# Column attention, first of four stages: symmetric scores from the diagonal on, x transposed by DMA, and the splitting of x spread over three engines

## The chip, the core and the metric

The program runs on one core of one Trainium2 chip. The metric is the device time of one execution in microseconds (us). An engine is called by the name of the profile: PE (TensorE matmul; PEld are its weight loads), DVE (VectorE), ACT (ScalarE), POOL (GpSimd), SP (SyncE, which only issues DMAs here).

## What is computed

Input x is 8 x 512 x 512 in float32. Four blocks follow, each of the form x = x + layernorm(block(layernorm(x))). The change is in the first block:

```python
scores = jnp.einsum('bci,bcj->bij', x, x)
weights = jax.nn.softmax(scores, axis=-1)
context = jnp.einsum('bij,bcj->bci', weights, x)
```

Each batch's score matrix is symmetric. The second block multiplies by the sum over eight 512 x 512 factors, and the first stage sums those factors on the side. The third block is grouped attention, the fourth a gated feed-forward layer.

## The kernel before

A batch is 4 tiles (T = 4) of 128 rows x 512 columns. Every product is made to nearly float32 accuracy by splitting each operand into a high part (fp32r, a rounded copy) and a low part (what is left), and adding three products: `products` (L57) issues 12 matmuls per output tile, three pairs for each of four blocks of the contraction.

`column_attention` is the first stage. Per batch b it makes the normalised xn (DVE, L335), its high part xh (DVE, L341) and low part xl (POOL, L231). PE makes four score tiles of 128 x 512 from them, in two PSUM banks used in turn (`score[t % 2]`). For each score tile DVE takes the row maximum, ACT the exponential, DVE the reciprocal of the row sum, POOL multiplies (prob, L236). PE transposes xn and prob in blocks of 128 x 128 into `turned` (L439), ACT takes the high part out of PSUM (xth, pth), DVE the low part (xtl, ptl, L357). From these PE makes four context tiles. For the residual, DVE takes the statistics of the context tiles (obn, omv), POOL turns them into a scale and a shift (`row_scales`, four small instructions), ACT applies them (normed, L301), POOL adds to x (L247). DVE also adds one 1 MB factor to `factor_sum` in each batch (L391).

Each engine has its own written-out order, and semaphores join them. A batch's context tiles run one batch behind its scores. Of a loop over pairs of batches (`over_batches`) PE, DVE and SP execute the body; ACT and POOL run their last steps two batches behind. DMAs are issued on SP alone. Within a batch PE's order is: score tile and transposes of xn, four times, then context tile of the batch before and transposes of prob, four times. The context buffers are four PSUM banks, so context tile t of a batch waits until ACT has read tile t of the batch before.

## Time and profile before

| | us |
|---|---|
| median of 3 runs (1651.66 to 1653.26) | 1653.04 |
| the profiled execution | 1653.88 |
| its span, first to last instruction | 1652.0 |
| PE busy / DVE busy / POOL busy in the span | 1498.8 / 1048.3 / 733.4 |

The times in the rows are counted from the first instruction of the span. Durations in a trace overlap for matmuls, since they are pipelined: what a matmul costs is read from start to start, not from its length. The first stage takes some 257 us of the span; the other three follow and are not changed.

### The profile page before, as it was taken

The page shows a single profiled execution, that of the slowest core. Times are in us where ns is not written, and L with a number is a line of the kernel's source. Part 1 is how long each engine was busy: PE and PEld are TensorE (multiplying, and loading weights), DVE is VectorE, ACT ScalarE, POOL GpSimd, SP SyncE. Part 2 cuts the span into 40 slices and gives each one's busy share as a digit, 9 for nine tenths or more (in the row PEclk, how much of TensorE's full clock was granted, in tenths as well). Part 3 has the DMA queues.
Part 4 walks back from the last instruction along what each step waited for, and adds up shares of the span by engine and source line. Part 5 has one row for each costly group of instructions (what it writes and reads, how often), then busy time and mean ns, then how long its engine had stood idle before and what let it go on. Part 6 is the DMA issues. An engine that isn't in the chain of part 4 may idle for free.

```text
span 1652.0 us, 22026 instructions
## 1 busy us (share of the span) xinstructions
PE 1498.8 (91%) x7332; PEld 1214.2 (73%) x7332; DVE 1048.3 (63%) x2091; ACT 789.7 (48%) x1506; POOL 733.4 (44%) x914
## 2 busy tenths in 40 slices
PE   4999996995899999999999998579899999999996
PEld 3777775874687877778787876467688888888885
DVE  4698846874888888888888778545424334234233
ACT  1333334644877878687878777321212222222121
POOL 3486742663444545454545445213243333333331
PEclk9999997997999999999999999889999999999998
DMA  4121102224000202020202020222110110100100
GB/s 152 52 102 51 50 1 71 76 89 141 1 1 1 77 1 77 2 77 1 77 1 77 1 96 1 83 96 90 33 51 1 51 51 0 51 32 18 51 26 26
DMA packets 41797, 80.00 MB, mean 48 GB/s; under 512 B 2416, under 2 KB 3440, under 8 KB 41712
## 3 DMA queue, kind: packets, MB, share of 16 engines
q1 hardware_dynamic: 41712, 78.93, 13.7%
q8 instruction: 46, 0.75, 0.2%
q14 instruction: 39, 0.32, 0.1%
HBM read 53.75 MB, written 25.17 MB: 48 GB/s over the span
## 4 chain that ended last, share of the span: by engine, by line
PE 57%; DVE 10%; POOL 4%; issue 3%; ACT 3%; DMA 1%; SPq 0%; POOLq 0%; DVEq 0%; ACTq 0%
PE f_inner L57 22%; PE g_side L1381 12%; PE f_down L1792 9%; PE g_score L57 5%; PE g_turned L1401 5%; DVE g_ptl L1305 2%; PE g_output L1427 2%; PE g_output L1429 2%; DVE g_neg_max L1291 2%; DVE f_wl L1716 1%; POOL g_prob L1016 1%; PE f_inner L1764 1%; POOL g_power L990 1%; DVE g_q L1220 1%; ACT g_pth L1167 1%
## 5 line engine op out<-in xcount | busy, mean ns | idle before, releaser
L1016 POOL TENSOR_SCALAR g_prob<-g_prob,g_inv_sum 128x512 f32<-128x512 f32 x256 | 178.7, 698 | 308.4 <-DVE g_inv_sum L1296 308.4
L57 PE MATMUL f_inner<-f_xth,f_wh 128*128 128x512 f32 x704 | 281.3, 400 | 15.8 <-DVE f_wl L1716 12.7
L57 PE MATMUL f_inner<-f_xtl,f_wh 128*128 128x512 f32 x704 | 279.5, 397 | 0.0
L1685 DVE SCALAR_TENSOR_TENSOR f_hidden<-f_inner,f_inner_scale,f_silu 128x512 f32<-128x512 f32 x88 | 66.0, 750 | 313.8 <-PE f_inner L57 313.8
L1574 POOL TENSOR_TENSOR f_hl<-f_hidden,f_hh 128x512 fp32r<-128x512 f32 x88 | 128.1, 1456 | 296.8 <-DVE f_hh L1691 296.8
L1626 ACT ACTIVATE f_silu<-f_inner,f_inner_scale 128x512 f32<-128x512 f32 x88 | 60.7, 690 | 413.8 <-PE f_inner L57 413.8
L1291 DVE TENSOR_REDUCE g_neg_max<-g_score 128x1 f32<-128x512 f32 x256 | 175.4, 685 | 83.9 <-PE g_score L57 82.7
L1125 ACT ACTIVATE g_prob<-g_score,g_neg_max 128x512 f32<-128x512 f32 x256 | 177.0, 691 | 96.9 <-DVE g_neg_max L1291 94.7
L1305 DVE TENSOR_TENSOR g_ptl<-g_turned,g_pth 128x512 fp32r<-128x512 f32 x256 | 173.8, 679 | 15.6 <-ACT g_pth L1167 13.6
L1401 PE MATMUL g_turned<-identity,g_prob 128*128 128x128 f32 x1024 | 155.2, 274 | 27.1 <-DVE g_ptl L1305 27.0
L57 PEld LDWEIGHTS f_inner<-f_xth,f_wh 128*128 128x128 f32 x704 | 133.1, 189 | 54.6 <-DVE f_wl L1716 17.5
L1167 ACT CAST g_pth<-g_turned 128x512 fp32r<-128x512 f32 x256 | 149.5, 584 | 46.7 <-PE g_turned L1401 44.6
L1401 PEld LDWEIGHTS g_turned<-identity,g_prob 128*128 128x128 f32 x1024 | 121.3, 140 | 64.3 <-issue 34.4
L57 PEld LDWEIGHTS f_inner<-f_xtl,f_wh 128*128 128x128 f32 x704 | 133.2, 189 | 31.7
L1792 PE MATMUL f_down<-f_wh,f_hh 128*128 128x512 f32 x352 | 140.1, 398 | 0.9 <-POOL f_hl L1574 0.9
L1792 PE MATMUL f_down<-f_wh,f_hl 128*128 128x512 f32 x352 | 139.3, 396 | 0.0
L57 PE MATMUL g_score<-g_kh,g_q 128*128 128x512 f32 x256 | 122.2, 478 | 2.7 <-DVE g_q L1220 2.7
L1427 PE MATMUL g_output<-g_pth,g_v 128*128 128x512 f32 x256 | 101.0, 395 | 1.6 <-DVE g_ptl L1305 1.6
L57 PE MATMUL g_score<-g_kl,g_q 128*128 128x512 f32 x256 | 100.9, 394 | 0.0
L1429 PE MATMUL g_output<-g_ptl,g_v 128*128 128x512 f32 x256 | 100.6, 393 | 0.0
L1792 PEld LDWEIGHTS f_down<-f_wh,f_hh 128*128 128x128 f32 x352 | 66.3, 188 | 16.9 <-POOL f_hl L1574 1.3
L1792 PEld LDWEIGHTS f_down<-f_wh,f_hl 128*128 128x128 f32 x352 | 66.4, 189 | 15.5
(200 smaller groups left out, 3460.3 us busy)
## 6 DMA issues: line engine op xcount, KB each, us to landing
x_resident<-x SPq DMA_DIRECT2D x8, 1024.0 KB, 7.0
x_mixed<-x_resident SPq DMA_DIRECT2D x8, 1024.0 KB, 4.4
x_pair<-x_mixed SPq DMA_DIRECT2D x8, 1024.0 KB, 7.8
g_res<-x_mixed SPq DMA_DIRECT2D x8, 1024.0 KB, 6.1
x_attended<-g_res SPq DMA_DIRECT2D x8, 1024.0 KB, 5.1
x_pair<-x_attended SPq DMA_DIRECT2D x8, 1024.0 KB, 5.7
factor<-factors SPq DMA_DIRECT2D x7, 1024.0 KB, 5.2
out<-x_pair SPq DMA_DIRECT2D x7, 1024.0 KB, 4.3
```

What stands on the lines that cost most here:

```text
L57: last = nc.tensor.matmul(out, lhsT, rhs, start=(n == 0), stop=(n == len(pairs) - 1))
L1016: nc.gpsimd.tensor_scalar(prob[:, at, :], prob[:, at, :], inv_sum[:, at:at + 1], 1.0, ALU.mult, ALU.mult).then_inc(prob_ready, 1)
L1125: nc.scalar.activation(prob[:, at, :], score[u % 2][:, :], ACT.Exp, bias=neg_max[:, at:at + 1], scale=1.0, accum_out=row_sum[:, at:at + 1] ...
L1167: nc.scalar.copy(pth[:, (turn_u // T) % 2, :, at * P:(at + 1) * P], blocks_of(turned[turn_u % 2][:, :])).then_inc(hi_ready, 1)
L1291: nc.vector.reduce_max(neg_max[:, at:at + 1], score[u % 2][:, :], AX, negate=True).then_inc(max_ready, 1)
L1305: nc.vector.tensor_tensor(ptl[:, at, :, cols], blocks_of(turned[turn_u % 2][:, :]), pth[:, at, :, cols].bitcast(F32), ALU.subtract).then_i ...
L1381: last = nc.tensor.matmul(out[:, bank_cols], *pairs[n], start=(k == 0 and n == 0), stop=(k == T - 1 and n == 2))
L1401: mm = nc.tensor.transpose(turned[turn_u % 2][:, cols], prob[:, turn_u % 4, cols], s.identity[:, :])
L1427: nc.tensor.matmul(output[hd % 2][:, :], lhsT, pth[:, hd % 2, t, :], start=(t == 0), stop=False)
L1429: mm = nc.tensor.matmul(output[hd % 2][:, :], lhsT, ptl[:, hd % 2, t, :], start=False, stop=(t == T - 1))
L1574: nc.gpsimd.tensor_tensor(hl[:, at, :], hidden[:, at, :], hh[:, at, :].bitcast(F32), ALU.subtract).then_inc(hl_ready, 1)
L1792: last = nc.tensor.matmul(down[t][:, :], l[:, at, cols], r[:, i, 2, :], start=(i == 0 and n == 0), stop=(i == IT - 1 and n == len(halves) ...
```

## The change

The names and lines are those of the new kernel. A DRAM input `x_t` holds each batch transposed; it is made ahead of the run.

- Scores: tile t is computed only from column 128 t on (512, 384, 256, 128 columns). ACT copies what stands right of the diagonal block into SBUF (`upper`), and PE transposes those blocks into the columns left of the diagonal of later tiles (1, 2 and 3 transposes).
- xn is not stored. ACT makes xh from x directly (scale and shift in one activation); POOL makes `scaled` = x times scale; DVE makes xl = scaled + shift - xh in one instruction with two SBUF inputs.
- The transposes of xn on PE, with their PSUM reads, go. `x_t` comes by DMA in two halves per batch into `xt`; ACT makes xth, DVE makes xtl from `xt` and xth, both in SBUF.
- A factor is loaded and added in two halves. The residual's statistics and scales go by pairs of tiles. The context of a batch is normed one batch behind instead of two. PE's order interleaves score and context tiles. The loops are written out.

The diff, cut to its core (removed bodies stand in the listing above):

```diff
-        xn = sb("xn", [P, 2, T, N])
+        scaled = sb("scaled", [P, T, N])
+        xt = sb("xt", [P, T, N])
...
         prob = sb("prob", [P, T, N])
+        upper = [sb(f"upper{t}", [P, N - (t + 1) * P]) for t in range(T - 1)]
         normed = sb("normed", [P, 2, N])
-        factor = sb("factor", [P, T, N])
...
+            load_x(0)
+            for b in range(B):
+                if b < B - 1:
+                    sp.wait_ge(x_loaded, b * 16 + 16)
+                    load_x(b + 1)
+                for h in range(2):
+                    load_half(b, h)
...
                 else:
...
-
+                    for h in range(2):
+                        if b > 1 or h > 0:
+                            sp.wait_ge(factor_used, b * 2 - 2 + h)
+                        sp.dma_start(factor[:, :, :], rows_of(factors, b)[:, 2 * h:2 * h + 2, :]).then_inc(factor_loaded, 16)
         @block.gpsimd
...
+                nc.gpsimd.tensor_scalar(raw_eps[:, b % T, :], mv[:, :, 1], EPS, EPS, ALU.add, ALU.mult)
...
+            def scaled_x(b, tiles):
+                if tiles[0] == 0:
+                    pool.wait_ge(scales, b + 1)
...
+                    nc.gpsimd.tensor_scalar(scaled[:, t, :], s.x[:, b * T + t, :], rs[:, t:t + 1], 1.0,
+                                            ALU.mult, ALU.mult).then_inc(scaled_ready, 1)
...
+            def output_scales(b, h):
+                half = slice(2 * h, 2 * h + 2)
+                pool.wait_ge(ostats, b * 2 + h + 1)
...
             scales_of(0)
...
+            scaled_x(0, range(T))
+
+            def body(b, p, first, last):
+                if b >= 2:
+                    add(b - 2, 0)
+                    output_scales(b - 2, 1)
+                    add(b - 2, 1)
+                    add(b - 2, 2)
+                probabilities(b, p, 0)
+                if last:
+                    following.row_scales(nc, s, pool)
+                else:
+                    scales_of(b + 1)
+                probabilities(b, p, 1)
                 if not last:
-                    for t in range(T):
-                        lo_of(b + 1, 1 - p, t)
-
-            over_batches_two_behind(pool, body)
-            output_scales(B - 2)
-            for t in range(T):
+                    scaled_x(b + 1, (0, 1, 2))
+                probabilities(b, p, 2)
+                if not last:
+                    scaled_x(b + 1, (3,))
+                if b >= 2:
+                    add(b - 2, 3)
+                if not first:
+                    output_scales(b - 1, 0)
+                probabilities(b, p, 3)
...
+            def hi_of_xn(b, p, t):
+                if t == 0:
+                    act.wait_ge(scales, b + 1)
+                    if b >= 2:
+                        act.wait_ge(scored, (b - 1) * T)
+                nc.scalar.activation(xh[:, p, t, :], s.x[:, b * T + t, :], ACT.Identity, bias=shift[:, t:t + 1],
+                                     scale=rs[:, t:t + 1]).then_inc(xh_ready, 1)
+
+            def copy_upper(b, t):
+                act.wait_ge(scored, b * T + t + 1)
+                nc.scalar.copy(upper[t][:, :], score[t % 2][:, (t + 1) * P:]).then_inc(copied, 1)
...
+            def hi_of_xt(b, p, t):
+                if t % 2 == 0:
+                    act.wait_ge(xt_loaded[t // 2], b * 16 + 16)
...
+                nc.scalar.copy(xth[:, p, t, :], xt[:, t, :]).then_inc(xth_ready, 1)
...
+            def body(b, p, first, last):
+                hi_of_xt(b, p, 0)
+                hi_of_xt(b, p, 1)
+                copy_upper(b, 0)
+                if not first:
+                    hi_of_prob(b - 1, 1 - p, 2)
+                    hi_of_prob(b - 1, 1 - p, 3)
+                if b >= 2:
+                    norm(b - 2, 2)
+                exp(b, p, 0)
+                copy_upper(b, 1)
+                if b >= 2:
+                    norm(b - 2, 3)
+                exp(b, p, 1)
+                copy_upper(b, 2)
+                if not last:
+                    hi_of_xn(b + 1, 1 - p, 0)
+                exp(b, p, 2)
+                if not last:
+                    hi_of_xn(b + 1, 1 - p, 1)
+                hi_of_prob(b, p, 0)
+                if not last:
+                    hi_of_xn(b + 1, 1 - p, 2)
+                hi_of_prob(b, p, 1)
+                exp(b, p, 3)
+                if not last:
+                    hi_of_xn(b + 1, 1 - p, 3)
+                if not first:
+                    norm(b - 1, 0)
+                    norm(b - 1, 1)
+                hi_of_xt(b, p, 2)
+                hi_of_xt(b, p, 3)
+                if last:
+                    hi_of_prob(b, p, 2)
+                    hi_of_prob(b, p, 3)
...
+            def lo_of_xn(b, p, t):
+                dve.wait_ge(scaled_ready, b * T + t + 1)
+                dve.wait_ge(xh_ready, b * T + t + 1)
+                nc.vector.scalar_tensor_tensor(out=xl[:, p, t, :], in0=scaled[:, t, :], scalar=shift[:, t:t + 1],
+                                               in1=xh[:, p, t, :].bitcast(F32), op0=ALU.add,
+                                               op1=ALU.subtract).then_inc(xl_ready, 1)
+
+            def lo_of_xt(b, p, t):
+                dve.wait_ge(xth_ready, b * T + t + 1)
+                nc.vector.tensor_tensor(xtl[:, p, t, :], xt[:, t, :], xth[:, p, t, :].bitcast(F32),
+                                        ALU.subtract).then_inc(xtl_ready, 1)
...
             def maximum(b, p, t):
                 dve.wait_ge(scored, b * T + t + 1)
+                if t < T - 1:
+                    dve.wait_ge(copied, b * (T - 1) + t + 1)
                 nc.vector.reduce_max(neg_max[:, p * T + t:p * T + t + 1], score[t % 2][:, :], AX,
                                      negate=True).then_inc(max_ready, 1)
...
+                if t % 2 == 1:
+                    h = t // 2
+                    tile.then_inc(own_obn, 1)
+                    dve.wait_ge(own_obn, b * 2 + h + 1)
+                    if b > 0:
+                        dve.wait_ge(oscales, b * 2 + h - 1)
+                    for t in (2 * h, 2 * h + 1):
                         last = nc.vector.bn_aggr(omv[:, t, :], obn[:, t, :])
                     last.then_inc(ostats, 1)
...
+            def add_factor(b, h):
+                dve.wait_ge(factor_loaded, 16 + ((b - 1) * 2 + h + 1) * 16)
+                half = s.factor_sum[:, 2 * h:2 * h + 2, :]
+                nc.vector.tensor_tensor(half, half, factor[:, :, :], ALU.add).then_inc(factor_used, 1)
...
             def body(b, p, first, last):
...
+                if b >= 2:
+                    output_stats(b - 2, 3)
                 if not last:
-                    hi_of_xn(b + 1, 1 - p)
-                for t in range(T):
-                    if not first:
-                        output_stats(b - 1, t)
-                    lo_of(b, p, T + t)
-
-            over_batches(dve, body)
-            dve.wait_ge(added, T + 2)
-            following.statistics(nc, dve, [s.x[:, t, :] for t in range(T)])
-            for t in range(T):
+                    tile_stats(b + 1, 0)
+                    tile_stats(b + 1, 1)
+                    tile_stats(b + 1, 2)
+                if not first:
+                    lo_of_prob(b - 1, 1 - p, 2)
+                    lo_of_prob(b - 1, 1 - p, 3)
+                maximum(b, p, 0)
+                if not last:
+                    tile_stats(b + 1, 3)
+                    stats_of(b + 1)
+                if last:
+                    dve.wait_ge(added, T)
+                    following.statistics(nc, dve, [s.x[:, t, :] for t in range(T)])
+                inverse(b, p, 0)
+                maximum(b, p, 1)
+                lo_of_xt(b, p, 0)
+                if not first:
+                    output_stats(b - 1, 0)
+                    add_factor(b, 0)
+                inverse(b, p, 1)
+                lo_of_xt(b, p, 1)
+                maximum(b, p, 2)
+                if not last:
+                    lo_of_xn(b + 1, 1 - p, 0)
+                inverse(b, p, 2)
+                if not last:
+                    lo_of_xn(b + 1, 1 - p, 1)
+                if not first:
+                    output_stats(b - 1, 1)
+                lo_of_prob(b, p, 0)
+                maximum(b, p, 3)
+                lo_of_prob(b, p, 1)
+                if not last:
+                    lo_of_xn(b + 1, 1 - p, 2)
+                inverse(b, p, 3)
+                if not last:
+                    lo_of_xn(b + 1, 1 - p, 3)
+                if not first:
+                    output_stats(b - 1, 2)
+                lo_of_xt(b, p, 2)
+                lo_of_xt(b, p, 3)
+                if not first:
+                    add_factor(b, 1)
+                if last:
+                    lo_of_prob(b, p, 2)
+                    lo_of_prob(b, p, 3)
...
+            written_out(body)
+            output_stats(B - 2, 3)
+            for t in range(T - 1):
                 output_stats(B - 1, t)
-
-            for t in range(T):
-                dve.wait_ge(ctx_normed, B * T + t + 1)
-                x = tile_of(s.x, (B - 1) * T + t)
-                nc.vector.tensor_tensor(x, x, normed[:, t % 2, :], ALU.add).then_inc(last_added, 1)
+            add_last(0)
+            add_last(1)
+            output_stats(B - 1, 3)
+            add_last(2)
+            add_last(3)
 
...
                 if not (first and t < 2):
                     pe.wait_ge(exp_ready, b * T + t - 1)
...
+                if t > 0:
+                    pe.wait_ge(copied, b * (T - 1) + t)
+                for r in range(t):
+                    nc.tensor.transpose(score[t % 2][:, block_at(r)], upper[r][:, block_at(t - r - 1)],
+                                        s.identity[:, :])
+                products(nc, score[t % 2][:, t * P:],
+                         [(l[:, p, k, block_at(t)], r[:, p, k, t * P:])
                           for k in range(T) for l, r in ((xh, xh), (xl, xh), (xh, xl))]).then_inc(scored, 1)
...
+                pe.wait_ge(prob_ready, b * T + g + 1)
...
                 if t == 0:
-                    pe.wait_ge(lo_ready, (b + 1) * 8)
-                pe.wait_ge(ctx_normed, b * T + t + 1)
-                at = slice(t * P, (t + 1) * P)
+                    pe.wait_ge(xtl_ready, (b + 1) * T)
+                    pe.wait_ge(lo_ready, (b + 1) * T)
+                if b > 0:
+                    pe.wait_ge(ctx_normed, (b - 1) * T + t + 1)
...
+                scores(b, p, 0, first)
+                if not first:
+                    turn(b - 1, 1 - p, 2, b == 1)
+                    turn(b - 1, 1 - p, 3, b == 1)
+                scores(b, p, 1, first)
+                if not first:
+                    contexts(b - 1, 1 - p, 0)
+                scores(b, p, 2, first)
+                if not first:
+                    contexts(b - 1, 1 - p, 1)
+                turn(b, p, 0, first)
+                scores(b, p, 3, first)
+                turn(b, p, 1, first)
+                if not first:
+                    contexts(b - 1, 1 - p, 2)
+                if last:
+                    turn(b, p, 2, first)
+                    turn(b, p, 3, first)
+                if not first:
+                    contexts(b - 1, 1 - p, 3)
+
+            written_out(body)
             for t in range(T):
```

In the order of instructions, DVE in the middle of a steady batch stood like this before (`xn` and `xtl` belong to the next batch and this one):

```order
L391 TENSOR_TENSOR factor_sum<-factor_sum,factor 128x2048
L350 RECIPROCAL inv_sum<-row_sum 128x1
L345 TENSOR_REDUCE neg_max<-score 128x1
L354 REGISTER_ALU
L357 TENSOR_TENSOR xtl<-turned,xth 128x4x128
L335 TENSOR_SCALAR xn<-x_resident,mv,rs 128x512 x2
L350 RECIPROCAL inv_sum<-row_sum 128x1
```

And now, from the statistics of the first context tile on:

```order
L437 BN_STATS obn<-context 128x6
L451 TENSOR_TENSOR factor_sum<-factor_sum,factor 128x1024
L427 RECIPROCAL inv_sum<-row_sum 128x1
L415 TENSOR_TENSOR xtl<-xt,xth 128x512
L422 TENSOR_REDUCE neg_max<-score 128x1
L409 SCALAR_TENSOR_TENSOR xl<-scaled,shift,xh 128x512
L427 RECIPROCAL inv_sum<-row_sum 128x1
L409 SCALAR_TENSOR_TENSOR xl<-scaled,shift,xh 128x512
L437 BN_STATS obn<-context 128x6
L445 BN_AGGR omv<-obn 128x2 x2
```

The factor's addition is halved, and instructions that read two SBUF operands (xtl, xl) stand between the maxima and the reciprocals.

POOL, from the second probability tile of a steady batch to the fourth, now stands like this (before, an addition to x followed each probability tile, and four `xl` ended the batch):

```order
L249 TENSOR_SCALAR prob<-prob,inv_sum 128x512
L244 TENSOR_SCALAR scaled<-x_resident,rs 128x512 x3
L249 TENSOR_SCALAR prob<-prob,inv_sum 128x512
L244 TENSOR_SCALAR scaled<-x_resident,rs 128x512
L265 TENSOR_TENSOR x_resident<-x_resident,normed 128x512
L255 TENSOR_TENSOR ove<-omv,raw_eps 128x2
L256 TENSOR_SCALAR oshift<-omv 128x2
L258 TENSOR_TENSOR ors<-ove,minus_half 128x2
L260 TENSOR_TENSOR oshift<-oshift,ors 128x2
L249 TENSOR_SCALAR prob<-prob,inv_sum 128x512
```

The scales of the first pair of context tiles (ove to oshift) now stand behind the scaled tiles and ahead of the last probability tile.

## Rows read from the trace of the kernel before

**Rows 1.** Busy time by window, one batch: length, engines, PE clock, DMA share, GB/s.

```profile
125.80:152.50 26.70, 26.11 (x129) 21.10 (x128) 22.93 (x42) 10.20 (x20) 19.26 (x20) 1.00 0.22 79
```

**Rows 2.** Timeline of PE in a steady batch: start, us, what.

```profile
72.07 0.60 PE L439 MATMUL turned<-identity,prob 128*128 128x128 f32 x4
72.43 0.48 PE L57 MATMUL score<-xh 128*128 128x512 f32 x1
72.74 0.39 PE L57 MATMUL score<-xh,xl 128*128 128x512 f32 x1
...
75.28 0.60 PE L439 MATMUL turned<-identity,xn 128*128 128x128 f32 x4
```

**Rows 3.** Timeline of PE in the third stage: fp32r matmuls with 128 moving columns.

```profile
398.04 0.28 PE L1381 MATMUL g_side<-g_wvl,g_hth 128*128 128x128 f32 x1
...
402.95 0.28 PE L1381 MATMUL g_side<-g_wvh,g_htl 128*128 128x128 f32 x1
```

**Rows 4.** Groups by line in 20 to 250 us: busy, mean ns, idle before.

```profile
L335 DVE TENSOR_SCALAR xn<-x_resident,mv,rs 128x512 f32 x24 | 26.1, 1126 | 1.6 <-POOL shift L108 1.6
L282 ACT ACTIVATE prob<-score,neg_max 128x512 f32<-128x512 f32 x32 | 22.1, 692 | 21.0 <-DVE neg_max L345 21.0
L345 DVE TENSOR_REDUCE neg_max<-score 128x1 f32<-128x512 f32 x32 | 21.7, 678 | 27.2 <-PE score L57 27.2
L292 ACT CAST pth<-turned 128x512 fp32r<-128x512 f32 x32 | 18.8, 587 | 60.4 <-PE turned L439 60.4
L391 DVE TENSOR_TENSOR factor_sum<-factor_sum,factor 128x2048 f32<-128x2048 f32 x7 | 16.0, 2282 | 0.0
```

**Rows 5.** Instructions of POOL's lines L236 and L247: count, ns min/median/max.

```profile
L236 POOL TENSOR_SCALAR prob<-prob,inv_sum x32: 687/702/1802, 29.9 to 220.4; 128x512 f32<-128x512 f32 x32
L247 POOL TENSOR_TENSOR x_resident<-x_resident,normed x28: 1269/1447/1468, 85.1 to 239.0; 128x512 f32 x16, 128x512 f32<-128x512 f32 x12
```

**Rows 6.** Timeline of DVE and POOL where both use SBUF.

```profile
161.52 2.28 DVE L391 TENSOR_TENSOR factor_sum<-factor_sum,factor 128x2048 f32<-128x2048 f32 x1
161.71 2.18 POOL L104 TENSOR_SCALAR shift<-mv 128x4 f32<-128x4 f32 x1
...
138.59 1.29 POOL L247 TENSOR_TENSOR x_resident<-x_resident,normed 128x512 f32 x1
138.62 2.40 DVE L335 TENSOR_SCALAR xn<-x_resident,mv,rs 128x512 f32 x2 [0.26 <-POOL shift L108]
```

**Rows 7.** Timeline of the start: DVE, and PE's first matmuls of batches 0, 1, 7.

```profile
7.43 2.47 DVE L324 BATCH_NORM_STATS2 bn<-x_resident 128x6 f32<-128x512 f32 x4 [7.43 <-DMA x_resident<-x]
...
12.38 1.91 DVE L335 TENSOR_SCALAR xn<-x_resident,mv,rs 128x512 f32<-128x512 f32 x4 [2.07 <-POOL shift L108]
...
19.28 0.76 PE L57 MATMUL score<-xh 128*128 128x512 f32 x1 [19.28 <-POOL xl L231]
24.54 1.05 PE L439 MATMUL turned<-identity,xn 128*128 128x128 f32 x4
...
44.56 0.79 PE L57 MATMUL score<-xh 128*128 128x512 f32 x1 [3.03 <-POOL xl L231]
...
205.73 0.47 PE L57 MATMUL score<-xh 128*128 128x512 f32 x1
```

**Rows 8.** Windows: the first score tile of batch 1, and the initial loads.

```profile
44.50:49.60 5.10, 5.04 (x12) 3.94 (x13) 0.00 (x0) 0.00 (x0) 0.00 (x0) 0.52 0.01 3
...
8.00:20.00 12.00, 0.72 (x2) 0.66 (x3) 6.74 (x18) 0.00 (x0) 6.19 (x6) 1.00 0.72 262
```

**Rows 9.** Timeline of the stage's end and the start of the second stage.

```profile
235.32 0.77 PE L57 MATMUL context<-pth,xth 128*128 128x512 f32 x1 [3.70 <-ACT normed L301]
...
248.50 0.39 PE L57 MATMUL context<-ptl,xth 128*128 128x512 f32 x1
...
252.09 2.99 ACT L301 ACTIVATE normed<-context,oshift,ors 128x512 f32<-128x512 f32 x4 [13.51 <-POOL oshift L108]
257.05 1.97 PE L695 MATMUL turned<-identity,xn 128*128 128x128 f32 x8 [8.16 <-ACT xn L574]
```

More of the change, by code:

```diff
@@ L166, in column_attention @@
         shift = sb("shift", [P, T])
+        raw_eps = sb("raw_eps", [P, T, T])
         obn = sb("obn", [P, T, 6])
@@ L244, in add @@
             def add(b, t):
-                pool.wait_ge(ctx_normed, b * T + t + 1 + T)
-                x = tile_of(s.x, b * T + t)
+                pool.wait_ge(ctx_normed, b * T + t + 1)
+                x = s.x[:, b * T + t, :]
                 nc.gpsimd.tensor_tensor(x, x, normed[:, t % 2, :], ALU.add).then_inc(added, 1)
             scales_of(0)
-            for t in range(T // 2):
-                lo_of(0, 0, t)
-            pool.sem_inc(xl_ready, T // 2)
-            def body(b, p, before, last):
-                if before == 2:
-                    output_scales(b - 2)
-                for t in range(T):
-                    normalise(b, p, t)
-                    if t == 0 and not last:
-                        scales_of(b + 1)
-                    if before == 2:
-                        add(b - 2, t)
-                if not last:
-                    for t in range(T):
-                        lo_of(b + 1, 1 - p, t)
@@ L318, in _, with tile_stats @@
+            written_out(body)
+            norm(B - 2, 2)
+            norm(B - 2, 3)
+            for t in range(T):
+                norm(B - 1, t)
         @block.vector
         def _(dve):
-            def stats_of(b, p):
-                dve.wait_ge(x_loaded[p], (b - p) * 8 + 16)
-                for t in range(T):
-                    last = nc.vector.bn_stats(bn[:, t, :], tile_of(s.x, b * T + t))
-                last.then_inc(own_bn, 1)
-                wait_alone(dve, s, own_bn, b + 1)
+            def tile_stats(b, t):
+                if t == 0:
+                    dve.wait_ge(x_loaded, b * 16 + 16)
+                tile = nc.vector.bn_stats(bn[:, t, :], s.x[:, b * T + t, :])
+                if t == T - 1:
+                    tile.then_inc(own_bn, 1)
@@ L360, in output_stats, with lo_of_prob @@
-            def output_stats(b, t):
-                dve.wait_ge(ctx_ready, (b + 1) * T + t + 1)
-                last = nc.vector.bn_stats(obn[:, t, :], context[t][:, :])
-                if t == T - 1:
-                    last.then_inc(own_obn, 1)
-                    wait_alone(dve, s, own_obn, b + 1)
-                    for t in range(T):
+            def lo_of_prob(b, p, g):
+                dve.wait_ge(hi_ready, b * T + g + 1)
+                nc.vector.tensor_tensor(ptl[:, p, :, block_at(g)], blocks_of(turned[g % 2][:, :]),
+                                        pth[:, p, :, block_at(g)].bitcast(F32), ALU.subtract).then_inc(lo_ready, 1)
```

202 lines of the change are left out of this document (75 added, 127 removed).

## The prediction

> **What bounds the kernel now.** I cut the first stage into batches by busy time per window, then read PE's timeline, the groups by line and the timelines of the other engines around them. In a steady batch PE is busy 26.1 of 26.7 us, DVE 22.9, POOL 19.3, ACT 10.2 [rows 1]. So PE ends the batch, with DVE close behind: only what shortens PE counts, and only until DVE or POOL ends last. Between the first score tiles of batches 1 and 7 lie 161.2 us for six batches, 26.9 each [rows 7].
>
> PE's costs are read from start to start. A 128 x 512 fp32r matmul takes 0.231 us (11 from 72.74 to 75.28), 0.31 as the first of a tile behind transposes; four transposes take 0.36 us [rows 2]. A tile is 12 matmuls, 2.85 us, and 3.2 with its transposes; eight make 25.7 us. With 128 moving columns a matmul takes (402.95 - 398.04)/44 = 0.112 us [rows 3].
>
> **PE in the new kernel.** The widths 384 and 256 do not occur in this trace. They lie between 0.112 and 0.231 us; the straight line between these gives 0.191 and 0.151, which I take since both ends are measured and the cost cannot grow with fewer columns. A batch is then:
> - scores: 12 x (0.231 + 0.191 + 0.151 + 0.112) = 8.2 us, where 11.1 were;
> - six transposes out of `upper`: 6 x 0.09 = 0.5;
> - context tiles: 48 x 0.231 = 11.1; first matmuls behind a switch, 8 x 0.08 = 0.6;
> - four transposed prob tiles 4 x 0.36 = 1.4; the four of xn are gone.
>
> Sum 21.8 us, with 20.4 to 24.7 as ends (all three narrow widths at 0.112, or at 0.231).
>
> The Trainium skill ("TensorE: Matmul & The Clock Gate", back-to-back issue gap) gives N/2.4 + 2.5 ns for an isolated matmul, 56 ns at 128 columns, and 81 ns in a stream with weight loads. The row of 0.112 us disagrees with both. By the formula the three narrow tiles would be 1.5 us shorter, PE's batch 20.3 us, and the sum below would not move except in batches 0 and 7, since another chain ends the batch.
>
> **The other engines.** DVE per batch, from the rows of its old work [rows 4]: eight statistics and four maxima of 0.68 to 0.69, four ptl of 0.68, eight new subtractions (xl, xtl) with two SBUF inputs at about 0.68 (a quarter of the 2.28 us of the factor's addition is 0.57, the old xtl took 0.68), two half additions of 1.14, small ones 1.8: 20.5 us, where 22.9 were. Gone are four xn at 1.13 and four casts. POOL: eight scalings at 0.70 and four additions at 1.27 [rows 5], three sets of scales at 1.9: 16.4 us; its four xl go. ACT gets four activations at 0.75 (one quarter of 2.99) [rows 9], three copies below 0.59 and stays at some 16 us. None alone exceeds PE's 21.8, but they wait for each other.
>
> I walk that ring, each step beginning as the one before ends. Time 0 is DVE at the statistics of the last context tile of two batches back:
> - DVE: statistics and aggregation 1.1, three statistics 1.8, two ptl 1.3, maximum 0.65: 4.9. ACT's exponential 0.9: 5.8. DVE: second maximum behind ACT's copy of `upper` to 6.9, xtl 0.6, statistics 0.6, half factor 1.1, reciprocal 0.1: 9.3.
> - POOL: prob 0.7, three scaled 2.1, prob 0.7, scaled 0.7, addition 1.3, scales of the first pair 1.9: 16.7.
> - ACT: two normed 1.5, a cast 0.6; DVE: two xtl 1.3, half factor 1.1: 21.2.
>
> Nothing in it waits for PE. Added to it: about 0.4 us of semaphore latencies (most waits in such a chain end 0.05 to 0.1 us late) and the SBUF conflict. That one is in the rows: POOL's shift, 0.23 us elsewhere, lasts 2.18 us while DVE adds the factor, and DVE's two xn, 1.0 us for two at the start (1.91 for four [rows 7]), last 2.40 us beside POOL's 1.29 us addition [rows 6]. On the ring five of POOL's instructions meet an xtl or xl of DVE; at 0.15 to 0.3 us each that is 1.2 us. The ring is 22.8 us: 1.0 us more than PE. I take 22.8 for the period. Its ends are PE's 21.8 and, if each of DVE's eight new SBUF instructions (0.68) and the two half additions (1.14) kept POOL off for its whole length, POOL's 16.4 + 7.7 = 24.1, and some 0.5 to 1 of dependent waits on top.
>
> **What is hidden.** The x_t transfers add 8 x 1 MB. The queue moved 262 GB/s in the initial stretch [rows 8], 4 us per MB; a batch has 3 MB, 12 us of 22.8. The halves of x_t are asked for when the last xtl of their half is done, ten and more us ahead of their use. If that cover went, up to 4 us per batch would show. Copying `upper` (about 0.5 us behind each score tile) lies beside context tiles on PE from batch 1 on; in batch 0 nothing covers it.
>
> **Start.** x lands at 7.43 us, statistics end at 10.3, scales (one more small instruction) at about 12.7 where xn started at 12.38 [rows 7]. Then ACT's four xh, POOL's scaled and DVE's xl run as a pipeline: 0.8 to the first, then four xl of 0.68 with SBUF conflicts, some 3.6: first score tile at 17.1 instead of 19.28. It runs at half clock as before (5.3 us from 19.28 to 24.54 [rows 7]): 22.4. Copy 0.7; second tile 2.9 (part of it cold) 26.0; copy 0.6, third 2.0: 28.6; transposes; fourth to 30.8; transposes, cast, exponential, xh 3, xl 3 (0.35 + 0.8 + 0.9 + 0.75 + 0.7 with latencies): batch 1 starts at 34.3, where it was 44.56. The gain is 10.3 us. PE idles 3.1 us ahead of it. Behind the old 3.03 us of idling the granted clock of the next tile was 0.52, the 1.2 GHz level [rows 8], so I charge batch 1 again 12 x (0.43 - 0.23) = 2.4 us: 24.2 us.
>
> **Batches 1 to 7.** 24.2 + 5 x 22.8 = 138.2 instead of 161.2: 23.0 gained.
>
> **End.** Before, the last scores start at 205.73 and the last context matmul ends at 248.9; on the way PE waits 3.70 us for norms and then runs a tile cold [rows 9]. Now batch 7's own two extra transposes make 22.5, lateness of the ring 1.0, four last context tiles 11.4: 34.9 instead of 43.2. The old norms (three quarters of an us each, four in a row) are now two behind the last tile: of the 8.16 us to the second stage's first transposes [rows 9] 1.3 to 1.6 go. Together 9.6.
>
> **Sum.** 10.3 + 23.0 + 9.6 = 42.9 us. Against the profiled execution's 1653.9 that is 1611.0; the median of the runs is 0.8 lower: 1610.
>
> **Rivals.**
> - PE still ends the batch (period 21.8; the conflict is milder than charged). For it: POOL's prob has a median of 0.702 against a minimum of 0.687 [rows 5], so most such work runs undisturbed. Against it: the ring of 22.8. Five periods and the lateness: 6.5 us less, 1603.5.
> - The SBUF conflict decides: of POOL and a DVE instruction with two SBUF inputs one stands still for the whole length of the other, as POOL's shift does behind the factor's addition [rows 6]. A period of 24.6 to 25.5 follows (24.1 above and the dependent waits), 5 x 2.2 = 11 us more and one on the start: 1622. Against it: two xn and an addition, 2 x 0.5 and 1.29 us alone, took 2.40 together [rows 6], no more than their sum, and POOL's additions have a median of 1.45 for 1.27 [rows 5]. The Trainium skill ("SBUF — State Buffer", two separate sides) states this as a rule: an exclusive lock on a shared port pair, held for the whole instruction. The trace agrees for the factor's addition.
> - Narrow matmuls cost as much as wide ones, so that the change does not do what it says: PE 24.7, period 24.7, also 1622. Against it: 0.112 us at 128 columns.
> - Slower than before: the new chain of score tile, copy, maximum, exponential leaves PE idle for 3 us in each batch. As between batches 0 and 1, a tile at half clock follows. From 21.8 us, 3.0 + 2.4 make 27.2, plus copy waits; it decides from an idle gap of about 3 us, which the old kernel had twice, with 5.3 us tiles behind both. Six such batches with two gaps each (32.6) give 6 x (32.6 - 22.8) = 59 more: 1669. Against it: from batch 1 on each tile of scores has a context tile or transposes beside it, and the walk shows PE stalls of at most 1 us.
>
> **How the numbers follow.** The ring at 22.8: 0.50, 1610. PE-bound: 0.19, 1603.5. SBUF port: 0.21, 1622. Narrow as wide: 0.06, 1622. Slower: 0.04. The range takes in both ends of the period: below PE-bound less 2.5 for the start, 1601; above 1623. A change within 0.2% (3.3 us, about what this kernel's measurement can tell) would need 40 us of errors on one side: 0.01. Faster 0.95, slower 0.04.
>
> **What would show it.** The starts of the first score tiles of batches 2 to 7 give the period: 22.8 by the ring, with PE idle about 1 us per batch ahead of a context tile or of the next scores, waiting for DVE (ptl or xl); 21.8 without such waits if PE-bound; over 24 with POOL and DVE instructions of twice their length by the port. Batch 1 starts at 34.3. PE at 384 and 256 columns shows 0.19 and 0.15 us from start to start. DVE's xl and xtl last 0.6 to 0.7 undisturbed. The gap between last context tile and second stage is below 7 us. The prediction is wrong if the walk has missed a wait on PE, above all ahead of a score tile (copy of `upper`) or if the granted clock drops within the batches.

## The result: 1606.67 us, and the profile after

The new kernel takes 1606.67 us, median of 4 runs (1605.33 to 1607.67), against 1653.15 for the one before: ratio 0.9718, 95% interval 0.9701 to 0.9735. Forecast were 1610, between 1601 and 1623. The page of the profiled execution:

```profile
span 1604.3 us, 21640 instructions
PE 1458.3 (91%) x7252; PEld 1190.4 (74%) x7252; DVE 1029.6 (64%) x2064; ACT 820.6 (51%) x1562; POOL 717.8 (45%) x956
```

PE's timeline gives the first score tiles of batches 0, 1, 2 and 7, the first context tile behind the last scores, and the second stage's first transposes (answering to [rows 7, 9]):

```profile
17.05 0.77 PE L57 MATMUL score<-xh 128*128 128x512 f32 x1 [17.05 <-DVE xl L409]
...
35.98 0.76 PE L57 MATMUL score<-xh 128*128 128x512 f32 x1 [5.35 <-issue]
...
58.78 0.39 PE L57 MATMUL score<-xh 128*128 128x512 f32 x1
...
168.63 0.39 PE L57 MATMUL score<-xh 128*128 128x512 f32 x1
...
191.91 0.47 PE L57 MATMUL context<-pth,xth 128*128 128x512 f32 x1 [1.18 <-issue]
...
209.05 0.48 PE L815 MATMUL turned<-identity,xn 128*128 128x128 f32 x1 [5.99 <-ACT xn L694]
```

Three differences from before account for the gain: start 44.56 - 35.98 = 8.6 us; batches 1 to 7 161.2 - 132.65 = 28.5; end 51.3 - 40.4 = 10.9. Their sum is 48.0, and the span is 47.7 shorter. Batches 2 to 6 take 21.8 to 22.03 us each.

The three later stages, which nothing here changes, take 1395.2 us of this execution and 1394.1 to 1401.4 us of those of the experiments; the third alone takes 680.3 to 684.8. So a few us between two medians need not come from the first stage, and the start of the second stage is the better measure of it.

One steady batch by window (columns as in [rows 1]), and the waits from batch 3 to 7 (engine, tile, line, what it waited for: us in total, times, longest):

```profile
102.59:124.59 22.00, 21.24 (x119) 18.34 (x118) 19.31 (x38) 14.23 (x28) 16.98 (x26) 1.00 0.44 144
```
```profile
DVE xtl L415 <- ACT xth L328: 5.9, 4, 1.5
PE context L57 <- issue: 3.1, 4, 0.8
DVE xl L409 <- POOL scaled L244: 2.7, 4, 0.7
```

PE waits 0.76 us once per batch, ahead of the first context tile. The profile puts it down to "issue", but the timelines of PE and DVE show what is late:

```profile
108.24 0.34 PE L57 MATMUL score<-xl,xh 128*128 128x384 f32 x1
109.34 0.47 PE L57 MATMUL context<-pth,xth 128*128 128x512 f32 x1 [0.76 <-issue]
```
```profile
102.94 1.31 DVE L415 TENSOR_TENSOR xtl<-xt,xth 128x512 fp32r<-128x512 f32 x2 [1.47 <-ACT xth L328]
104.18 1.21 DVE L451 TENSOR_TENSOR factor_sum<-factor_sum,factor 128x1024 f32<-128x1024 f32 x1
105.32 0.69 DVE L437 BATCH_NORM_STATS2 obn<-context 128x6 f32<-128x512 f32 x1
106.04 0.25 DVE L445 BATCH_NORM_AGGREGATE omv<-obn 128x2 f32<-128x6 f32 x2
106.20 1.85 DVE L393 BATCH_NORM_STATS2 bn<-x_resident 128x6 f32<-128x512 f32 x3
107.97 1.27 DVE L432 TENSOR_TENSOR ptl<-turned,pth 128x512 fp32r<-128x512 f32 x2
```

The last ptl ends at 109.24 and PE starts at 109.34. From 102.94 on DVE has no pause: the batch is late by DVE's wait of 1.47 us for xth, which ACT makes behind two norms that wait for POOL's `oshift`. That is the ring of the prediction. POOL's and ACT's part of it, in the batch that begins with DVE's statistics at 105.32:

```profile
114.41 1.05 POOL L249 TENSOR_SCALAR prob<-prob,inv_sum 128x512 f32<-128x512 f32 x1
```
```profile
122.97 1.45 ACT L340 ACTIVATE normed<-context,oshift,ors 128x512 f32<-128x512 f32 x2 [0.94 <-POOL oshift L260]
```

PE's widths, from start to start: 384 columns (108.24 - 106.48)/10 = 0.176 us, 256 columns (113.46 - 112.50)/8 = 0.120:

```profile
106.48 0.34 PE L57 MATMUL score<-xh,xl 128*128 128x384 f32 x1
...
112.50 0.28 PE L57 MATMUL score<-xh,xl 128*128 128x256 f32 x1
...
113.46 0.28 PE L57 MATMUL score<-xh 128*128 128x256 f32 x1
```

### The profile page after: what moved, and what is told of

It reads as the page before. It is cut to its first block, busy times and chain, and to the rows that moved or that the text cites. A ratio compares the mean times of both kernels' runs of the same rounds, so it can differ in the third digit from the quotient of the medians.

```text
span 1604.3 us, 21640 instructions
## 1 busy us (share of the span) xinstructions
PE 1458.3 (91%) x7252; PEld 1190.4 (74%) x7252; DVE 1029.6 (64%) x2064; ACT 820.6 (51%) x1562; POOL 717.8 (45%) x956
## 4 chain that ended last, share of the span: by engine, by line
PE 63%; DVE 10%; issue 2%; POOL 2%; ACT 1%; DMA 1%; SPq 0%; POOLq 0%; DVEq 0%; ACTq 0%
PE f_inner L57 22%; PE g_side L1501 15%; PE f_down L1912 9%; PE g_score L57 6%; PE g_turned L1521 6%; PE g_output L1547 2%; PE g_output L1549 2%; DVE g_ptl L1425 2%; DVE g_neg_max L1411 2%; DVE g_q L1340 1%; DVE f_wl L1836 1%; PE f_inner L1884 1%; DVE f_hidden L1805 1%; PE g_side L1471 0%; DVE g_obn L1359 0%
## 5 line engine op out<-in xcount | busy, mean ns | idle before, releaser
L1521 PE MATMUL g_turned<-identity,g_prob 128*128 128x128 f32 x1024 | 155.6, 274 | 26.1 <-DVE g_ptl L1425 26.1
```

What stands on the lines that cost most here:

```text
L1521: mm = nc.tensor.transpose(turned[turn_u % 2][:, cols], prob[:, turn_u % 4, cols], s.identity[:, :])
```

## Experiments

All but the seventh change the new kernel. "Period" is the time between first score tiles of neighbouring steady batches. All in us; the last two columns are of the profiled execution, of which each kernel has one:

| | median | profiled execution | second stage starts |
|---|---|---|---|
| kernel before | 1653.15 | 1653.88 | 257.05 |
| new kernel | 1606.67 | 1606.05 | 209.05 |
| 1 | 1606.53 | 1604.05 | 208.19 |
| 2 | 1601.43 | 1605.48 | 204.20 |
| 3 | 1620.2 | 1624.08 | 220.91 |
| 4 | 1622.16 | 1621.95 | 221.71 |
| 5 | 1605.81 | 1605.81 | 207.62 |
| 6 | 1596.39 | 1600.86 | 199.32 |
| 7 | 1648.2 | 1647.29 | 251.00 |
| 9 | 1596.1 | 1596.23 | 199.83 |

The eighth has other work ahead of the stage.

**1. Casts ahead of the norms.**

```diff
+                hi_of_xt(b, p, 2)
+                hi_of_xt(b, p, 3)
                 if not first:
                     norm(b - 1, 0)
                     norm(b - 1, 1)
-                hi_of_xt(b, p, 2)
-                hi_of_xt(b, p, 3)
```

> ScalarE's last two high parts of x_t of a batch stand ahead of the two norms that wait for GpSimd, not behind them. Ring theory (DVE, GpSimd, ScalarE and DVE again set the 22.01 us between batches; PE itself needs 21.1): DVE's last two xtl no longer wait for GpSimd's scales, the ring falls under 21.1, PE's wait of 0.76 us ahead of the first context tile goes, and six batches give 5 to 6 us: 1601. PE theory (PE needs the 22.01 itself, the 0.76 us is its own issue time): no change, 1606.7.

Measured: 1606.53 us, ratio 0.9727 (0.9712 to 0.9742), no different from the new kernel, where 1601 was expected. The period fell to 21.58 and PE's wait to 0.42 in four batches; batches 1 and 2 took 1.4 us more than in the new kernel. DVE's wait for xth is gone, but most of it came back beside POOL:

```profile
101.60 2.44 DVE L415 TENSOR_TENSOR xtl<-xt,xth 128x512 fp32r<-128x512 f32 x2
```
```profile
102.02 1.47 POOL L265 TENSOR_TENSOR x_resident<-x_resident,normed 128x512 f32<-128x512 f32 x1 [0.22 <-ACT normed L340]
```

Two xtl took 1.31 us before and 2.44 now: POOL's addition runs over the second. The ring has a second way round, through SBUF, and takes back 1.1 of the 1.5 us.

**2. Without the second half addition** (the sum of the factors lacks its second half).

```diff
+                if h == 1:
+                    dve.sem_inc(factor_used, 1)
+                    return
```

> The second half addition of each factor (1.21 us of DVE) is left out, so the sum of the factors is incomplete; its load stays. Ring theory: it lies on the ring, which falls to 20.8 us, under PE's 21.1: period 21.1, 5 to 6 us less, 1601. PE theory: no change.

Measured: 1601.43 us, ratio 0.9682 (0.9663 to 0.97), the median of two runs at 1598.4 and 1598.5 and two at 1604.3 and 1605.5. The second stage starts 4.9 us earlier than in the new kernel. The period is 21.01 and PE no longer waits; so 21.0 is PE's own time:

```profile
101.88 0.39 PE L57 MATMUL score<-xh 128*128 128x512 f32 x1
...
122.89 0.39 PE L57 MATMUL score<-xh 128*128 128x512 f32 x1
```

**3. A second addition of the same length at that place.**

```diff
+                if h == 1:
+                    last = nc.vector.tensor_tensor(factor[:, :, :], factor[:, :, :], factor[:, :, :], ALU.add)
...
```

> Behind the second half addition DVE adds the loaded half once more onto itself, 1.2 us more of DVE with two SBUF inputs at the same place. Ring theory: the period grows by the whole 1.2 us to 23.2; seven batches, 8 us more, 1615. PE theory: DVE's lateness has 0.3 to 0.9 us of room first, at most 0.3 us a batch, 1609.

Measured: 1620.2 us, ratio 0.9796 (0.9781 to 0.9811), 5 us more than expected. The period grew to 23.14, by 1.1 for an instruction that starts 1.13 before its successor, and all of it stands as PE's wait, which went from 0.76 to 1.99:

```profile
113.42 0.47 PE L57 MATMUL context<-pth,xth 128*128 128x512 f32 x1 [1.99 <-issue]
```

Together with experiment 2 this shows that DVE's chain ends the batch, and not PE. The second stage starts 11.9 us later, not 8: batch 5 took 24.73 us, with a mean granted clock of 0.75 from 137.15 to 144.00 us, after batches in each of which PE had waited 2 us; and the stage's end took 4.0 us longer. The other 6.2 us of this profiled execution lie in the later stages.

**4. Scores at full width** (no copies, no transposes out of them).

```diff
-                products(nc, score[t % 2][:, t * P:],
+                products(nc, score[t % 2][:, :],
```

> All four score tiles with 512 columns again, no copies of upper and no transposes of it; everything else as in the new kernel. If the narrow widths are worth what their columns say (0.231, 0.176, 0.120, 0.112 us a matmul): PE 21.1 + 3.4 - 0.65 = 23.9 us a batch, above the ring, so PE sets the period without stalls: 1.9 x 6 plus some 4 in batches 0 and 7, 1622. Rival, that x_t by DMA brought nearly all of the gain and the ring would hide the wider tiles: under 1612.

Measured: 1622.16 us, ratio 0.9814 (0.9799 to 0.9829), as expected. The period is 23.63, and PE does not wait: 22.00 us busy in 22.00. In the new kernel the diagonal is worth 1.6 us per steady batch, 12.7 us by the start of the second stage and 15.5 by the medians.

**5. The addition out of the way as well** (ACT's order of experiment 1).

```diff
-                    add(b - 2, 0)
                     output_scales(b - 2, 1)
+                    add(b - 2, 0)
                     add(b - 2, 1)
```

> ACT's two casts of x_t go ahead of the two norms, as in the experiment before, and POOL's body now begins with the scales of the second pair, with the addition of tile 0 behind them, so that no POOL addition runs beside DVE's last two subtractions of x_t. Ring broken and port conflict avoided: these subtractions last 0.7 us each instead of 1.8 for the second, PE never waits ahead of the first context tile, the period is PE's own 21.0, and the time is that of the kernel without the second half addition, 1600 to 1602 us. Rival, the scales of the second pair come later or the addition meets another DVE instruction with two SBUF inputs and gives the same back: period 21.6 and 1605 to 1607 us, as the reordered casts alone gave.

Measured: 1605.81 us, ratio 0.9719 (0.9704 to 0.9733): the expected 1600 to 1602 was missed, and the rival's 1605 to 1607 met. The two xtl last 1.3 us again, and the period is 21.4 in most batches, but one batch takes 22.1 and PE still waits some 0.2 us for the last ptl. The second stage starts 1.4 us earlier than in the new kernel, less than the 5 us between the fastest and the slowest run of this kernel.

The trace shows one place where time was given back: POOL's power instruction `rs` of the next batch's scales, which stands ahead of the second prob tile. Here DVE's half addition starts first, and in the new kernel `rs` does. This experiment, then the new kernel:

```profile
112.76 1.20 DVE L451 TENSOR_TENSOR factor_sum<-factor_sum,factor 128x1024 f32<-128x1024 f32 x1
```
```profile
112.87 1.99 POOL L106 TENSOR_TENSOR rs<-ve,minus_half 128x4 f32<-128x4 f32 x1
```
```profile
112.98 1.25 DVE L451 TENSOR_TENSOR factor_sum<-factor_sum,factor 128x1024 f32<-128x1024 f32 x1
```
```profile
112.95 1.03 POOL L106 TENSOR_TENSOR rs<-ve,minus_half 128x4 f32<-128x4 f32 x1
```

In the nine traces of the new kernel and its variants, `rs` takes 1.99 to 2.08 us in all 22 cases in which the addition starts 0.03 to 0.11 us ahead of it, and 1.04 wherever the two overlap and `rs` leads by 0.026 us or more. With a lead of 0.022 or 0.023 us it took 2.12 in three cases of four. DVE's wait for `scaled` grows from 0.68 to 1.29 us with it. What the period would be without this was not tested.

**6. Batch 0 written out for itself, and the last two ptl of batch 7 ahead of the half addition** (on top of 5; POOL and DVE's part of it):

```diff
+                if first:
+                    scales_of(1)
+                    scaled_x(1, (0, 1))
+                    probabilities(0, 0, 0)
...
+                if first:
+                    for t in range(T):
+                        tile_stats(1, t)
+                    stats_of(1)
+                    maximum(0, 0, 0)
+                    lo_of_xn(1, 1, 0)
+                    inverse(0, 0, 0)
...
```

> As the run before, and besides: in batch 0 the statistics, scales, xh, scaled and xl of batch 1 are done between the score tiles, so that batch 1 starts behind the last score tile, its transposes and little else; in batch 7 the last two ptl go ahead of the half addition. Theory: batch 1 starts at 31 to 32 instead of 36.0, its first tile is no longer at half clock (2.9 us instead of 5), and the 1.2 us wait ahead of the first context tile of batch 7 goes: 7 to 8 us less than the run before, 1592 to 1594. Rival, DVE's added statistics ahead of the first maximum delay the second score tile's successors by as much as they save: batch 1 at 34 to 35, and 2 to 3 us less only, about 1598.

Measured: 1596.39 us, ratio 0.9668 (0.9653 to 0.9682): 9.4 us below experiment 5, and faster than both kernels. The 7 to 8 us expected of it came (8.3 by the start of the second stage); 1592 to 1594 was missed since it stood on the time expected of experiment 5.

```profile
30.09 0.47 PE L57 MATMUL score<-xh 128*128 128x512 f32 x1 [0.28 <-issue]
...
182.16 0.47 PE L57 MATMUL context<-pth,xth 128*128 128x512 f32 x1 [0.41 <-issue]
...
199.32 0.48 PE L867 MATMUL turned<-identity,xn 128*128 128x128 f32 x1 [6.00 <-ACT xn L746]
```

Batch 1 starts at 30.09 (36.35 in experiment 5), and the second stage at 199.32 instead of 207.62: 8.3 us earlier, of which 6.3 at the start, 0.9 in batches 1 to 6 and 1.1 from the first of the last scores on. The mean granted clock over the first tile and more of batch 1 is 0.67 in the new kernel, behind 5.35 us without a matmul, and 1.00 here, behind 0.28 (windows; new kernel first):

```profile
35.98:41.50 5.52, 5.52 (x22) 4.52 (x23) 2.89 (x5) 1.62 (x4) 0.00 (x0) 0.67 0.52 180
```
```profile
30.09:33.20 3.11, 3.10 (x15) 2.56 (x16) 2.52 (x5) 2.32 (x6) 1.17 (x2) 1.00 0.18 68
```

**7. The diagonal alone, on the kernel before** (the factor in two halves, to make room for the copies).

```diff
+                    if t < T - 1:
+                        act.wait_ge(scored, b * T + t + 1)
+                        nc.scalar.copy(upper[t][:, :], score[t % 2][:, (t + 1) * P:]).then_inc(copied, 1)
...
+                for r in range(t):
+                    nc.tensor.transpose(score[t % 2][:, r * P:(r + 1) * P],
+                                        upper[r][:, (t - r - 1) * P:(t - r) * P], s.identity[:, :])
+                products(nc, score[t % 2][:, t * P:],
```

> The kernel before with the scores from the diagonal on alone (copies of the upper blocks on ACT, transposes out of them on PE); the factor is loaded and added in halves, to make room for the copies. Everything else is as before: xn stored, transposed on PE, four xl on POOL. By the widths measured, 12 x (0.231 x 3 - 0.176 - 0.120 - 0.112) = 3.4 us of matmul go per batch and 0.5 of transposes come: PE 23.3 instead of 26.1. If PE still bounds, the period is about 24.1 and the time 1653 - 8 x 2.8 = 1631. If DVE, 22.9 us busy and now waiting for the copies too, ends the batch, the period is 25 to 26 and the time 1640 to 1648. Taken: DVE, 1640.

Measured: 1648.2 us, ratio 0.9973 (0.9964 to 0.9983), 4.4 us where 13 were expected. PE's work fell from 26.1 to 23.93 us per batch but the period only from 26.7 to 26.6, so that of the gain 2.5 us lie ahead of batch 1 and little in the steady batches (window of one batch, then PE's and POOL's rows at its end):

```profile
101.00:127.60 26.60, 23.93 (x136) 19.89 (x135) 23.48 (x43) 11.24 (x23) 19.16 (x20) 1.00 0.24 79
```
```profile
131.84 0.55 PE L441 MATMUL score<-identity,upper 128*128 128x128 f32 x3 [1.40 <-ACT upper L311]
148.28 0.49 PE L57 MATMUL score<-xh 128*128 128x512 f32 x1 [0.99 <-POOL xl L234]
```
```profile
139.24 2.93 DVE L347 CAST xh<-xn 128x512 fp32r<-128x512 f32 x4
141.85 6.17 POOL L234 TENSOR_TENSOR xl<-xn,xh 128x512 fp32r<-128x512 f32 x4
```

PE now waits for the copies and for the chain xn, xh (DVE), xl (POOL, 6.17 us for four, where the kernel before took 5.20 from 147.14). The matmuls saved turn into these waits. So the kernel before had a second chain almost as long as PE's: there POOL's four xl end at 152.34, and PE, whose transposes end at 152.57, begins the next batch at 152.59. The rest of the change alone (experiment 4) brings 31 us, the diagonal alone 4, both together 46.5: the diagonal pays only together with the rest. That it needs both, xl away from POOL's end of the batch and other tiles on PE beside the copies, is read from the two waits above; neither was tried alone.

**8. DVE and POOL on SBUF, by themselves**, ahead of the stage; four 128 x 512 instructions on each engine per step.

```diff
+            phases = [(0, 1), (1, 0), (1, 1), (2, 0), (2, 1), (1, 2), (1, 3)]
...
+                            last = nc.vector.tensor_tensor(out, xt[:, 0, :] if kind == 1 else score[0][:, :],
+                                                           xt[:, 1, :], ALU.subtract)
...
+                            last = nc.gpsimd.tensor_tensor(out, xt[:, 2, :], xt[:, 3, :], ALU.add)
```

> Ahead of the first stage of the new kernel, DVE and POOL each work four instructions of 128 x 512 in seven steps: DVE subtracts two SBUF operands alone; POOL scales by a constant alone; both at once; POOL adds two tensors alone; both at once; POOL scales while DVE subtracts with one operand in PSUM; POOL scales while DVE does a tensor_scalar with one SBUF operand. The time of this kernel is that of the new one and some 35 us. Exclusive use, held for an instruction's whole length: alone 0.67 (DVE), 0.69 and 1.27 (POOL), at once each engine's instructions follow start to start at the sum of both, 1.36 with the scaling and 1.95 with the addition. Shared use: at once the start to start of the longer one is below 80% of the sum. With an operand in PSUM, or with one operand only, both stay at their time alone by either.

Measured: 1639.42 us in a single run. Windows of the seven steps; the third to fifth numbers of busy time are DVE's, ACT's and POOL's:

```profile
4.70:7.30 2.60, 0.00 (x0) 0.00 (x0) 2.53 (x5) 0.00 (x0) 0.00 (x0) 1.00 0.00 0
7.30:9.80 2.50, 0.00 (x0) 0.00 (x0) 0.00 (x0) 0.00 (x0) 2.36 (x4) 1.00 0.00 0
9.80:14.15 4.35, 0.00 (x0) 0.00 (x0) 3.73 (x4) 0.00 (x0) 4.17 (x4) 1.00 0.00 0
14.15:19.10 4.95, 0.00 (x0) 0.00 (x0) 0.00 (x0) 0.00 (x0) 4.92 (x4) 1.00 0.00 0
19.10:26.10 7.00, 0.00 (x0) 0.00 (x0) 5.70 (x4) 0.00 (x0) 6.78 (x4) 1.00 0.00 0
26.10:28.60 2.50, 0.00 (x0) 0.00 (x0) 2.47 (x4) 0.00 (x0) 2.36 (x4) 1.00 0.00 0
28.60:31.90 3.30, 0.00 (x0) 0.00 (x0) 2.69 (x5) 0.00 (x0) 3.10 (x4) 1.00 0.00 0
```

From start to start DVE's subtraction takes 0.61 us alone and POOL's scaling 0.58; together each takes 1.02, 86% of the sum. POOL's addition takes 1.22 alone, and 1.67 beside the subtraction, 92% of the sum. (The expectation's 1.36 and 1.95 added up lengths in the trace, which overlap on one engine.) So two such instructions hardly overlap; the subtraction's length goes from 0.69 to 1.09 beside the scaling and to 1.75 beside the addition. With one DVE operand in PSUM both stay at their time alone. The instructions of the fifth step (ns min/median/max):

```profile
L202 DVE TENSOR_TENSOR xtl<-xt x4: 693/1745/1751, 19.2 to 23.2; 128x512 fp32r<-128x512 f32 x4
```
```profile
L218 POOL TENSOR_TENSOR xth<-xt x4: 1704/1706/1779, 19.2 to 24.3; 128x512 fp32r<-128x512 f32 x4
```

The last step missed its expectation: a DVE tensor_scalar with a single SBUF operand also conflicts. POOL's scaling goes from 0.58 to 0.75 us from start to start, and of the four tensor_scalar the first, which began ahead of POOL, is 0.43 us long and the others 0.83.

The stage behind this block is the new kernel's own, and yet its batches 4 to 6 took 22.5 to 22.7 us, each behind a batch in which `rs` took 2.00 to 2.12 us (experiment 5).

**9. The last two ptl ahead of the third statistics** (on top of 6).

```diff
                     tile_stats(b + 1, 1)
-                    tile_stats(b + 1, 2)
                 if not first:
                     lo_of_prob(b - 1, 1 - p, 2)
                     lo_of_prob(b - 1, 1 - p, 3)
+                if not last:
+                    tile_stats(b + 1, 2)
```

> As the run with the first batch written out, and in each batch DVE takes the last two ptl ahead of the third tile statistics of the next batch instead of behind them. In the run before PE waited 0.33 us in most batches ahead of the first context tile, for the last ptl. Theory: this wait goes, the period falls from 21.4 to PE's own 21.0 to 21.1, and the time by 6 x 0.33 = 2 us to 1594 to 1595. Rival, the third statistics now delay the maximum of the first score tile and the ring behind it, exponential, prob, transposes: the period stays at 21.4 with PE's wait at another tile, and the time at 1596 to 1597.

Measured: 1596.1 us, ratio 0.9654 (0.964 to 0.9669); the rival's time and period came. The period stays at 21.39. The ptl end as late as before, since DVE itself comes to them later:

```profile
122.06 1.27 DVE L461 TENSOR_TENSOR ptl<-turned,pth 128x512 fp32r<-128x512 f32 x2
123.43 0.47 PE L57 MATMUL context<-pth,xth 128*128 128x512 f32 x1
```
```profile
DVE xl L438 <- POOL scaled L244: 2.6, 2, 1.3
```

DVE's only large wait left, 1.3 us per batch, is xl behind POOL's `scaled`, which stands behind an `rs` of 1.99 us in each of these batches (experiment 5). That this makes the last 0.4 us of ring is read from the trace and was not tested.

## Why the prediction was right, step by step

- **What ends the batch.** The ring was forecast with PE waiting about 1 us per batch for DVE (ptl or xl). It waits 0.76 us for ptl; experiments 2 and 3 show the ring from both sides. The rival of a PE-bound batch (1603.5 forecast; five periods of 1.0 and a lateness of 1.0 make 6.0 less, not 6.5) would have the time of experiment 2, 1601, and is not what the kernel does.
- **What bounded the kernel before.** "Only what shortens PE counts, and only until DVE or POOL ends last" left out how near that point was: experiment 7 took 2.2 us of work from PE per batch and got 0.1 for it.
- **The period, 22.8.** Measured 22.0. DVE is busy 19.3 of it and waits 2.7: 1.5 for xth, 0.7 for `scaled`, 0.3 for xh. The walk was right in its order and 0.8 us too long. Its parts, between the starts shown above: from DVE's statistics to POOL's prob 9.1 (9.3 forecast), from there to ACT's norm 8.6 (7.4, and 8.6 with the conflict), from there to the next statistics 4.4 (4.5). The 0.4 us of latencies added on top were too much, since they already lie in these times. POOL's part came out by luck: beside xl and xtl it is longer by some 1.8 us and not 1.2 (an estimate, from the starts of the same instructions with and without company), but the scales of one pair take 1.44 undisturbed (106.37 to 107.81) where 1.9 was charged, and the others follow each other somewhat closer than their lengths.
- **PE's own 21.8.** Measured 21.0 (experiment 2). The straight line for the narrow widths was the error: 0.191 and 0.151 were charged, 0.176 and 0.120 measured, 12 x 0.046 = 0.55 us of the 0.8. From 512 to 256 columns the cost falls nearly in proportion to the columns; 256 columns cost little more than the 0.112 of 128 [rows 3]. Since the ring ended the steady batches, this moved nothing there. The 81 ns that "TensorE: Matmul & The Clock Gate" (the Trainium skill, back-to-back issue gap) gives for 128 columns in a stream with weight loads is not met by the 0.112.
- **Start, 10.3.** Measured 8.6. The first score tile came at 17.05 (17.1 forecast), but batch 1 at 35.98 instead of 34.3. The walk took the fourth exponential and the last xh and xl right behind PE's fourth tile. DVE had two xl, stretched to 1.17 and 1.10 us beside POOL, and a ptl queued ahead of the fourth maximum, which starts at 32.55, 2.3 us behind PE's fourth tile. Experiment 6 takes this queue apart and gains 6.3 us there.
- **Cold batch 1, 24.2.** It was PE's 21.8 and 2.4 for a tile at half clock, and it took 22.80, with PE busy throughout:

```profile
35.98:58.78 22.80, 22.80 (x118) 19.70 (x119) 17.61 (x35) 11.87 (x25) 12.01 (x18) 0.92 0.41 139
```

  So this batch was bound by PE, as forecast, and both terms were too large. PE was busy 21.48 us in batch 1 of experiment 6, at full clock, so the half clock cost 1.3 us here. That size varied: behind 5.47 us without a matmul the granted clock was 0.50 and not 0.67 over the first 5.5 us of batch 1 in experiments 1 and 2, and the batch took 23.64 and 23.96.
- **Batches 1 to 7, 138.2.** Measured 132.65: 5 x 0.83 from the period and 1.4 from the cold batch.
- **End, 9.6.** Measured 10.9: 34.4 instead of 34.9 to the last context matmul, and the gap to the second stage 2.2 us shorter instead of 1.3.
- **SBUF conflict, 1.2 on the ring.** Its kind was right, and in experiment 8 the exclusive rule of "SBUF — State Buffer" (the Trainium skill, two separate sides) is nearly met, at 86 to 92% of the sum. The rival at 1622 failed for another reason: it had each xl, xtl and half addition hold POOL off for its whole length, and most of them miss POOL's work. POOL was busy 17.0 us per batch, where 24.1 was the rival's. One reading used against this rival was incomplete: the 2.40 us of two xn [rows 6] saw not only POOL's 1.29 us addition but also its prob (0.87 us from 139.86) and the start of the next addition (140.69). The groups by line give xl and xtl (mean ns; xl takes 0.74 us undisturbed):

```profile
L409 DVE SCALAR_TENSOR_TENSOR xl<-scaled,shift,xh 128x512 fp32r<-128x512 f32 x28 | 26.8, 959 | 7.5 <-POOL scaled L244 5.4 <-ACT xh L308 2.0
L415 DVE TENSOR_TENSOR xtl<-xt,xth 128x512 fp32r<-128x512 f32 x32 | 22.0, 705 | 7.8 <-ACT xth L328 7.7
```

The errors of the parts (1.7 too much, 5.5 and 1.3 too little) leave 5.1 us of gain more than forecast; the profiled execution took 1606.05 us where the sum gave 1611.0. The mechanism was right. That the median of 1606.67 lies only 3.3 us from 1610 is partly luck: the start's error took off a quarter of the others', and the median lay 0.6 above the profiled execution and not 0.8 below.

## What to carry to other kernels

Ask of a shortened engine what else ends the stage: the diagonal alone removed over 2 us of PE work per batch and shortened the period by 0.1, and was worth 1.6 us per batch once the other engines' chains were short. A chain that crosses four engines is found by walking it, and tested by making one instruction of it vanish and appear twice; when a wait is removed from it, look for POOL and DVE meeting in SBUF, and for which of them starts first: 0.1 us can decide whether a small POOL instruction takes 1 or 2 us. Write the first and the last batch out for themselves: a steady order run on batch 0 cost 6 us here.

## What the hardware showed beyond expectation

DVE and POOL slow each other when both work in SBUF, in both directions: a subtraction takes 1.75 us for 0.69 beside an addition, which itself takes 1.70 for 1.26, and a tensor_scalar on DVE with one SBUF operand shows a part of it. POOL's power function takes 0.71 us on 128 x 2 and 1.04 on 128 x 4, and the latter 1.99 to 2.12 where DVE's half addition starts ahead of it, or at most 0.023 us behind it in three of four cases. The cost of fp32r matmuls falls with the columns down to 256 (0.231, 0.176, 0.120 us) and hardly below (0.112 at 128).
